# Taking the first four groups of products between the heads of the first search's second half, with a softmax for each half, and the second tile's row ahead

## The chip, the cores and the metric

The kernel runs on one core of a Trainium2 chip. The metric is the device time of one execution in microseconds (us), as the median of several runs. Engines: TensorE (PE), VectorE (DVE), ScalarE (ACT), GpSimd (POOL) and SyncE (SP). Each takes its own list of instructions in the order in which the program writes it, and waits on semaphores for the others.

## The reference, cut to what matters

A graph of 1250 nodes with 512 features and 21250 edges passes through four layers, each added to its input behind a layer norm: a graph convolution with batch norm and gelu, a memory layer with product keys, a second graph convolution, and one of eight 512 x 512 matrices per node. The change lies in the second:

```python
q = (x @ Wq + bq).reshape(-1, 8, 128)
q1, q2 = q[..., :64], q[..., 64:]
s1 = einsum('bhc,hnc->bhn', q1, keys[:, 0])      # 256 scores for each head
s2 = einsum('bhc,hnc->bhn', q2, keys[:, 1])
s1t, i1 = top_k(s1, 8);  s2t, i2 = top_k(s2, 8)
scores, best = top_k(all 64 sums of s1t and s2t, 8)
indices = (i1 * 256 + i2) at best                 # 8 heads x 8 rows of 65536
inner = einsum('bd,bhkd->bhk', x, w_down[indices])
vals = relu(inner) * softmax(scores)              # over the 8 of a head
out = einsum('bhk,bhkd->bd', vals, w_up[indices])
```

Each node needs 64 rows of `w_down` and 64 of `w_up`. The kernel holds them side by side, so that one gathered row is 4 KB.

## The kernel before

The nodes lie in 10 tiles of 128 (`NT`), a node to a partition. For each tile the memory layer has two stages.

The **search**. The tile's row is normalised (`y_stats`, `y_root`, `y_inv`, `y_norm`: VectorE and ScalarE in turn), TensorE flips it (`flip_y`, L1923), ScalarE copies it out of PSUM (`copy_yT`, L910). TensorE makes the queries of two heads at a time (`queries`, L1932), ScalarE copies them with their bias (`copy_q`, L948). TensorE makes a head's scores (L1943; L2096 in the first tile), ScalarE copies them (L955; L1038), VectorE finds the eight largest and their places (L1395 and L1400; L1544 to L1556). Then VectorE combines the heads and writes a list of indices (`idx`, L1449; L1598), ScalarE takes the exponentials (`exps`, L985), and VectorE divides by their sums (`softmax`, L1458 to L1462) to get `prob`.

The **groups**. GpSimd gathers the rows of a tile by its list (L702), 128 rows of 4 KB (512 KB) at a time, two gathers to a group, 32 groups to a tile (`NG`). The rows land in a ring of ten groups (`RING`); a slot is free again when TensorE has summed its group (`grp_done`). For each group VectorE multiplies the `w_down` halves by the normalised row `Y` and sums them into `inner` (two products, L1534, scaled by `prob`), ScalarE makes two diagonal matrices of the relu of `inner` (L1030), and TensorE sums diagonal times `w_up` half (L2081).

While a tile's groups run, the searches of the next tiles are spread between them: `Places` says ahead of which group `g` each engine does which step of a search. `FIRST` is the list for tile 1, whose search runs in the groups of tile 0; its steps with a negative `g` run ahead of group 0. Its queries stand at groups 0, 2, 6 and 8, head h's scores at 2h + 2, their copy one group later, and the maxima one group behind that. With sums at 19 its list of indices comes at group 25.

Tile 0's own search has nothing to hide behind. It is written out by hand. Its list of indices comes in two halves (`SHARES`), one for four heads each, and GpSimd starts to gather by the first. VectorE goes through the heads in pairs (`first_pair`): the even head from a copy that ScalarE made, the odd head straight from a PSUM bank `S1`. There is one such bank pair, so TensorE's scores for an odd head h wait until the places of head h - 2 are found:

```python
        if h == 1:
            pe.wait_ge(k.x1_done, 4)
        elif h % 2:
            pe.wait_ge(k.topk_done, h - 1)
```

On ScalarE this search is: `copy_q` for two heads, the copy of the even head's scores, four times over, with two gelus of the first layer (L886) behind the last `copy_q`; then `keep_y(0)` (L924), which writes `Y`, then the exponentials (L985), and the root of the out-degrees (L1052). A function of another kind (root, gelu, exponential) has an ACT_TABLE_LOAD in front of it. On TensorE it is `flip_y(0)`, four times queries and two heads' scores, then `flip_y(1)`.

Of the kernel before, what the change touches and what calls it, by code (L numbers as in the profile page):

```python
# [23 lines left out]
ALU = mybir.AluOpType  # L24
ACT = mybir.ActivationFunctionType
AX = mybir.AxisListType

P = 128
N = 1250
D = 512  # L30
E = 21250
NT = -(-N // P)
# [3 lines left out]
H = 8  # L36
NK = 256
HK = H * 8
# [30 lines left out]
GS = 2  # L69
SHARES = 2  # L70
NG = HK // GS
RING = 10
# [30 lines left out]
class Places:  # L103


    def __init__(self, y_stats, y_inv, y_norm, y_copy, y_keep, queries, q_lag, scores, s_lag, m_lag, sums):
        self.y_stats, self.y_root, self.y_inv, self.y_norm, self.y_flip = y_stats, y_stats, y_inv, y_norm, y_norm
        self.y_copy, self.y_keep = y_copy, y_keep
        self.queries, self.q_copy = queries, [q + q_lag for q in queries]
        self.scores = scores  # L110
        self.s_copy = [s + s_lag for s in scores]
        self.maxes = [s + s_lag + m_lag for s in scores]
        self.finds = [s + s_lag + m_lag + 1 for s in scores]
        self.sums, self.best, self.place, self.codes = sums, sums + 1, sums + 2, sums + 3
        self.match, self.rows, self.index, self.exps, self.softmax = sums + 4, sums + 5, sums + 6, sums + 5, sums + 11
# [2 lines left out]
STEADY = Places(-36, -32, -32, -28, 2, [8 * c - 28 for c in range(4)], 4, [4 * h - 24 for h in range(H)], 4, 3, 13)  # L118
LATER = {2 + 3 * i: 4 + i for i in range(NT - 4)}
W1_MEANS, W1_CENTRED, LATER_ADD = NG + 3, NG + 6, 3  # L120
FIRST = Places(-6, -4, -3, -1, 1, [0, 2, 6, 8], 1, [2 * h + 2 for h in range(H)], 1, 1, 19)
FINAL = Places(-36, -32, -32, -28, 2, [8 * c - 28 for c in range(4)], 4, [4 * h - 24 for h in range(H)], 4, 3, 13)
FINAL.codes, FINAL.match, FINAL.rows, FINAL.index = 15, 16, 16, 17
TABLES, ROUTES, ROUTED, HOSTS, LAST_HOST = 1, 4, 7, 12, 28
# [9 lines left out]
def groups_of(i):  # L134
    return NG if i < NT - 1 else NG_LAST
# [655 lines left out]
def act_program(act, k):  # L791
# [92 lines left out]
    def gelu(o, i0, i1):  # L884
        piece = k.outT[:, o * NPAD + i0 * P:o * NPAD + i1 * P]
        act.activation(piece, piece, ACT.Gelu, bias=k.bsc[:, FT + o:FT + o + 1],  # L886
                       scale=k.bsc[:, o:o + 1]).then_inc(k.gelu_done, 1)
# [20 lines left out]
    def copy_yT(i):  # L908
        act.wait_ge(k.yt_ready, i + 1)
        act.activation(k.yT[:, :], k.YT, copy).then_inc(k.yT_done, 1)  # L910
# [6 lines left out]
    def keep_y(i):  # L917
        if i >= 2:
            act.wait_ge(k.inner_ready, (i - 1) * NG)
        elif i:  # L920
            act.wait_ge(k.topk_done, H)
        else:
            act.wait_ge(k.x1_done, 4)
        act.activation(k.Y[i % 2], k.x[:, i * D:(i + 1) * D], ACT.Identity, bias=k.yco[:, i % 2 * 2 + 1:i % 2 * 2 + 2],  # L924
                       scale=k.yco[:, i % 2 * 2:i % 2 * 2 + 1]).then_inc(k.y_kept, 1)
# [52 lines left out]
    def keep_g(i):  # L978
        act.wait_ge(k.g_psum, i + 1)
        act.wait_ge(k.hco_ready, i + 1)  # L980
        act.activation(k.g[i % 3], k.TK[i % 2], copy, scale=k.hco[:, 0:1]).then_inc(k.g_kept, 1)

    def exps(i):
        act.wait_ge(k.exp_in, i + 1)
        act.activation(k.ex[:, :], k.sm[:, :], ACT.Exp).then_inc(k.exp_done, 1)  # L985

    def search_step(i, at, g):
# [14 lines left out]

    def tile(i):
        for g in range(groups_of(i)):
            if i and g == AfterTile(i).root:
                x_root(i - 1)
            if i and g == AfterTile(i).copy:
                copy_xf(i - 1)
            if i and g == AfterTile(i).keep:
                keep_g(i - 1)  # L1010
            for j, at, place in at_search(i, g):
                search_step(j, at, place)
            n = i * NG + g
            if n in WIDEN:
                widen(WIDEN[n])
            if n in SCALED:
                scale_sums(SCALED[n])
            if i == NT - 2 and g == TABLES:
                tables()
            if i == NT - 2 and g == ROUTED:  # L1020
                keep_routes()
            if i == NT - 1 and g == 0:
                act.wait_ge(k.routes_ready, 1)
            act.wait_ge(k.inner_ready, n + 1)
            act.wait_ge(k.grp_done, n + 1 - DB + RING)
            for s in range(GS):
                j = g * GS + s
                c = (n % DB) * GS + s
                to = k.ident[:, :] if i < NT - 1 else k.routes[:, j // WIDTH * P:(j // WIDTH + 1) * P]
                ins = act.activation(k.diag[:, c * P:(c + 1) * P], to, ACT.Relu,  # L1030
                                     scale=k.inner[:, j:j + 1])
            ins.then_inc(k.diag_ready, 1)

    def first_scores(h):
        act.wait_ge(k.s_ready, h + 1)
        if h >= 4:
            act.wait_ge(k.topk_done, h - 3)
        act.activation(k.sc[h // 2 % 2].rearrange("p (c n) -> p c n", c=2), k.S[:, :, 0:NK], copy).then_inc(k.sc_ready, 1)  # L1038

    y_root(0)  # L1040
    y_norm(0)
    copy_yT(0)
    for c in range(4):
        copy_q(0, c)
        if c == 3:
            gelu(2, 4, NT)
            gelu(3, 4, NT)
        first_scores(2 * c)
    keep_y(0)
    exps(0)  # L1050
    act.wait_ge(k.dego_ready, 1)
    act.activation(k.dsq[:, 2 * NT:3 * NT], k.deg[:, 2 * NT:3 * NT], ACT.Sqrt).then_inc(k.degosq_ready, 1)  # L1052
    for g in range(FIRST.y_root, 0):
        search_step(1, FIRST, g)
    for i in range(NT):
        tile(i)
    copy_xf(NT - 1)
# [43 lines left out]
def dve_program(dve, k):  # L1101
# [351 lines left out]
                                     ALU.mult, ALU.add).then_inc(k.rows_known, 1)  # L1453

    def softmax(i):
        dve.wait_ge(k.exp_done, i + 1)
        ex = k.ex[:, :].rearrange("p (h a) -> p h a", a=8)
        dve.tensor_reduce(k.ssum[:, 0:H], ex, AX.X, ALU.add)  # L1458
        dve.drain()
        dve.reciprocal(k.ssum[:, H:2 * H], k.ssum[:, 0:H])  # L1460
        dve.drain()
        dve.tensor_tensor(k.prob[:, (i % 2) * HK:(i % 2 + 1) * HK].rearrange("p (h a) -> p h a", a=8), ex,  # L1462
                          k.ssum[:, H:2 * H].unsqueeze(2).to_broadcast([P, H, 8]), ALU.mult)
        dve.drain()
        if i == NT - 1:
            dve.sem_inc(k.weights_known, 1)
# [10 lines left out]
    def search_step(i, at, g):  # L1477
# [22 lines left out]
        if g == at.softmax:  # L1500
            softmax(i)

    def tile(i):
        for g in range(groups_of(i)):
            n = i * NG + g
            if i and g == AfterTile(i).add:
                x_add(i - 1)
            if i and g == AfterTile(i).stats:
                x_stats(i - 1)
            if i and g == AfterTile(i).inv:  # L1510
                x_inv(i - 1)
            if n in UNIT_ADD:
                add_unit(UNIT_ADD[n])
            if n - LATER_ADD in LATER:
                add_gelu(LATER[n - LATER_ADD])
            if n == W1_CENTRED:
                center_w1()
            for j, at, place_ in at_search(i, g):
                search_step(j, at, place_)
            r = n % RING  # L1520
            if i == NT - 2 and g == GATHERED:
                keep_rows()
            if i == NT - 2 and g == WEIGHTED:
                keep_weights()
            if g == 0:
                if i < NT - 1:
                    dve.wait_ge(k.y_kept, i + 1)
                else:
                    dve.wait_ge(k.y_hosted, 2)
            dve.wait_ge(k.landed[r], (n // RING + 1) * (16 * GS))  # L1530
            for s in range(GS):
                j = g * GS + s
                row = k.slot[r * GS + s][:, 0:D]
                ins = dve.tensor_tensor_reduce(  # L1534
                    out=row, in0=row, in1=k.Y[i % 2] if i < NT - 1 else k.Yh[j // WIDTH],
                    scale=k.prob[:, (i % 2) * HK + j:(i % 2) * HK + j + 1], scalar=0.0, op0=ALU.mult, op1=ALU.add,
                    accum_out=k.inner[:, j:j + 1])
            ins.then_inc(k.inner_ready, 1)

    def first_pair(h):  # L1540
        dve.wait_ge(k.sc_ready, h // 2 + 1)
# [60 lines left out]
    y_inv(0)  # L1602
    for i in range(1, 4):
        add_gelu(i)
    for b in range(SHARES):
        first_pair(4 * b)
        first_pair(4 * b + 2)
        first_part(b)
    sums_of = k.best[:, :].rearrange("p (h a) -> p h a", a=8)
    dve.tensor_tensor(k.sm[:, :].rearrange("p (h a) -> p h a", a=8), sums_of,  # L1610
                      sums_of[:, :, 0:1].to_broadcast([P, H, 8]), ALU.subtract).then_inc(k.exp_in, 1)
    dve.sem_inc(k.sc_ready, H // 2)
    softmax(0)
    dve.wait_ge(k.degosq_ready, 1)
    dve.reciprocal(k.dri[:, 2 * NT:3 * NT], k.dsq[:, 2 * NT:3 * NT])
    dve.drain()
    for g in range(FIRST.y_stats, 0):
        search_step(1, FIRST, g)
    for i in range(NT):
        tile(i)  # L1620

# [126 lines left out]
def pe_program(pe, k):  # L1748
# [353 lines left out]
    for c in range(4):  # L2102
        queries(0, c)
        first_scores(2 * c)
        first_scores(2 * c + 1)
    for g in range(FIRST.y_flip, 0):
        search_step(1, FIRST, g)
    for i in range(NT):
        tile(i)

# [113 lines left out]
```

## Time and profile before

| | |
|---|---|
| median of 3 runs | 1150.19 us (1150.16 to 1151.8) |
| the profiled execution's own time | 1151.4 us |
| its span, first to last instruction | 1149.2 us |
| mean granted TensorE clock | 0.98 |
| busy share: PE, DVE, ACT, POOL | 94%, 75%, 39%, 59% |
| gathers: L702 on POOL | 628, 944 to 952 ns each |

The page cuts the span in 40 slices of 28.7 us. Tile 0's search and the first gathers lie at 195 to 258 us, in slices 6 to 8 counted from 0. In a timeline a row is: start, us, engine, line and operation, out<-in by names, count, and in brackets the engine's idle time before it and what ended that. A row with a count above one is the sum over the instructions merged into it, from the first one's start to the last one's end. Times are us from the span's start. The granted clock of 1.00 is 2.4 GHz, that of 0.50 is 1.2 GHz.

### The profile page before, as it was taken

Reading aid. Unit: us, or ns where it says so; the run is one execution under the profiler, and the core shown is the slowest. Engines: PE = TensorE matmul, PEld = TensorE weight load, DVE = VectorE, ACT = ScalarE, POOL = GpSimd, SP = SyncE. Lnnn points to the kernel's source line nnn. Section 1 sums busy time; section 2 is a strip of 40 time slices with the busy share of each in tenths; the row PEclk is TensorE's granted clock in tenths of the full one; section 3 lists DMA queues with packets and bytes.
Section 4 is the critical chain, followed back from the end, with each engine's and each line's share of the span. In section 5 each row is a group of like instructions: output and inputs, shape, how many; then the busy total and the mean of one; then the engine's idle time right before and its main releaser. Section 6 shows DMA issues by size and latency. Waiting matters only on the chain.

```text
span 1149.2 us, 15190 instructions
## 1 busy us (share of the span) xinstructions
PE 1086.0 (94%) x3724; PEld 579.5 (50%) x3725; DVE 862.7 (75%) x2753; ACT 453.5 (39%) x1119; POOL 677.9 (59%) x751
## 2 busy tenths in 40 slices
PE   7989998489999999999999999999999989998998
PEld 3568887355444554454444544544544434343543
DVE  6757766769989988789788789798798796664411
ACT  3731114344444544444434434434434333353222
POOL 2010004477677777777777776777776777777322
PEclk9989999889999999999999999999999999999899
DMA  8960011499999999999999999999999999994822
GB/s 319 406 261 2 2 31 81 156 410 385 384 408 400 409 409 409 408 409 408 409 408 409 409 408 409 408 409 409 408 409 380 410 409 409 409 406 151 287 83 89
DMA packets 108439, 379.96 MB, mean 331 GB/s; under 512 B 11850, under 2 KB 12656, under 8 KB 108228
## 3 DMA queue, kind: packets, MB, share of 16 engines
q0 software_dynamic: 92272, 334.49, 73.6%
q1 hardware_dynamic: 16084, 44.51, 10.4%
q8 instruction: 33, 0.54, 0.2%
q14 instruction: 50, 0.41, 0.1%
HBM read 351.88 MB, written 27.93 MB: 330 GB/s over the span
## 4 chain that ended last, share of the span: by engine, by line
PE 61%; DVE 14%; DMA 9%; POOL 6%; issue 4%; DVEq 2%; ACT 2%; SPq 0%; POOLq 0%; ACTq 0%
PE tr L2081 28%; DMA big<-in_wdu,idx 7%; PE acc L1861 6%; PE acc L1973 5%; POOL big L702 5%; PE acc L1932 4%; DVE big L1534 4%; PE acc L1943 3%; PE tr L2166 2%; PE acc L1792 2%; DMA AT<-in_wdu,idx 2%; PE acc L2166 2%; PE acc L1815 1%; POOL AT L702 1%; PE tr L1965 1%
## 5 line engine op out<-in xcount | busy, mean ns | idle before, releaser
L702 POOL DMA_INDIRECT big<-in_wdu,idx x504 | 475.7, 944 | 188.9 <-issue 137.6
L2081 PE MATMUL tr<-big,back 128*128 128x512 f32 x1008 | 463.7, 599 | 14.2 <-ACT back L1030 13.9
L1534 DVE CUSTOM_DVE_ANT_0 big<-big,acc,prob 128x512 f32<-128x512 f32 x504 | 353.9, 742 | 82.8 <-DMA big<-in_wdu,idx 80.7
L1030 ACT ACTIVATE back<-ident,inner 128x128 f32<-128x128 f32 x576 | 199.4, 393 | 407.9 <-DVE inner L1534 407.7
L2081 PEld LDWEIGHTS tr<-big,back 128*128 128x128 f32 x1008 | 184.2, 190 | 249.8 <-issue 196.6
L702 POOL DMA_INDIRECT AT<-in_wdu,idx x124 | 118.1, 952 | 41.6 <-issue 33.6
L2081 PE MATMUL tr<-AT,back 128*128 128x512 f32 x248 | 115.1, 598 | 1.5 <-ACT back L1030 1.4
L1534 DVE CUSTOM_DVE_ANT_0 AT<-AT,acc,prob 128x512 f32<-128x512 f32 x124 | 87.3, 743 | 23.1 <-DMA AT<-in_wdu,idx 22.7
L1861 PE MATMUL acc<-AT,big 128*128 128x256 f32 (+1 forms) x400 | 91.2, 379 | 0.0
L1973 PE MATMUL acc<-front 128*128 128x512 f32 x188 | 88.7, 597 | 0.6 <-issue 0.5
L1932 PEld LDWEIGHTS acc<-front 128*128 128x128 f32 x640 | 78.2, 195 | 19.1 <-issue 17.1
L1932 PE MATMUL acc<-front 128*128 128x128 f32 x640 | 81.0, 281 | 1.6 <-ACT front L910 1.4
L1861 PEld LDWEIGHTS acc<-AT,big 128*128 128x128 f32 x400 | 75.7, 194 | 7.3
L2081 PEld LDWEIGHTS tr<-AT,back 128*128 128x128 f32 x248 | 45.4, 190 | 59.4 <-issue 47.3
L673 POOL TENSOR_TENSOR AT<-AT,ident 128x128 f32<-128x128 f32 x10 | 4.8, 476 | 103.3 <-ACT AT L813 103.3
L1395 DVE MAX8 top<-back 128x8 f32<-128x256 f32 x144 | 53.8, 416 | 10.4 <-ACT back L955 10.4
L1400 DVE FIND_INDEX8 topi<-top,back 128x8 uint32<-128x256 f32 x144 | 58.5, 419 | 0.0
L1973 PEld LDWEIGHTS acc<-front 128*128 128x128 f32 x188 | 34.7, 190 | 43.2 <-issue 42.6
L1534 DVE DVE_READ_ACCUMULATOR2_ANT inner<- 128x1 f32 x628 | 52.2, 83 | 0.0
L1943 PE MATMUL acc<-front 64*128 64x256 f32 x288 | 50.6, 428 | 0.0
L955 ACT ACTIVATE back<-acc 128x512 f32<-128x512 f32 x72 | 42.1, 585 | 3.4 <-PE acc L1943 3.4
L1226 DVE TENSOR_SCALAR back<-big 128x320 f16 x88 | 22.9, 302 | 27.0 <-PE acc L1815 10.2
(334 smaller groups left out, 1082.5 us busy)
## 6 DMA issues: line engine op xcount, KB each, us to landing
sorted_rows<-big SPq DMA_DIRECT2D x33, 640.0 KB, 18.7
big<-in_we SPq DMA_DIRECT2D x8, 1024.0 KB, 13.7
big<-in_wdu,idx POOLq DMA_INDIRECT x504, 10.2
x<-sorted_rows SPq DMA_DIRECT2D x13, 257.5 KB, 2.8
x<-in_x SPq DMA_DIRECT2D x1, 2304.0 KB
big<-in_xt SPq DMA_DIRECT2D x2, 1024.0 KB, 8.8
front<-in_wq SPq DMA_DIRECT2D x1, 2048.0 KB, 7.8
AT<-in_wdu,idx POOLq DMA_INDIRECT x124, 10.3
```

The source lines that it names most:

```text
L702: pool.indirect_dma_start(out=k.slot[r * GS + s], out_offset=None, in_=k.wdu_d, in_offset=bass.IndirectOffsetOnAxis(ap=k.idx[i % 2][:, j:j ...
L955: act.activation(k.sc[h % 2].rearrange("p (c n) -> p c n", c=2), k.S[:, :, 0:NK], copy).then_inc(k.sc_ready, 1)
L1030: ins = act.activation(k.diag[:, c * P:(c + 1) * P], to, ACT.Relu, scale=k.inner[:, j:j + 1])
L1395: dve.max(k.top[:, c * HK + h * 8:c * HK + h * 8 + 8], k.sc[h % 2][:, c * NK:(c + 1) * NK])
L1400: ins = dve.max_index(k.topi[:, c * HK + h * 8:c * HK + h * 8 + 8], k.top[:, c * HK + h * 8:c * HK + h * 8 + 8], k.sc[h % 2][:, c * NK:(c ...
L1534: ins = dve.tensor_tensor_reduce(out=row, in0=row, in1=k.Y[i % 2] if i < NT - 1 else k.Yh[j // WIDTH], scale=k.prob[:, (i % 2) * HK + j:(i ...
L1861: ins = pe.matmul(k.banks[2 + p % 4][:, 0:n], k.xw[:, t * D + o * P:t * D + (o + 1) * P], k.AT[:, t * NPAD + c0:t * NPAD + c0 + n], start= ...
L1932: ins = pe.matmul(k.Q[:, (h % 4) * P:(h % 4 + 1) * P], k.wq[:, f * H * P + h * P:f * H * P + (h + 1) * P], k.yT[:, f * P:(f + 1) * P], sta ...
L1943: ins = pe.matmul(k.S[:, c, 0:NK], k.qT[half, (h % 4) * P:(h % 4 + 1) * P], k.keys[half, h * NK:(h + 1) * NK], start=True, stop=True)
L1973: return pe.matmul(bank, counts[:, t % 4 * P:(t % 4 + 1) * P], k.g[j % 3], start=begin, stop=end)
L2081: ins = pe.matmul(k.O[i % 2], k.diag[:, c:c + P], row, start=(g == 0 and s == 0), stop=(g == groups_of(i) - 1 and s == GS - 1))
L2166: return pe.matmul(k.E[part], k.zT[part][:, f * P:(f + 1) * P], k.big[:, bass.ds(b * (FT * D) + f * D, D)], start=(f == 0), stop=(f == FT ...
```

## The change

`FIRST` loses its steps ahead of group 0 and its first two queries. They are written out by hand, inside the first search:

- VectorE does `y_stats(1)` and `y_inv(1)` and the reciprocal of the out-degrees' root ahead of the first pair of heads. ScalarE does `y_root(1)`, that root, and `y_norm(1)` ahead of the first `copy_q`.
- ScalarE does `copy_yT(1)` behind the last `copy_q(0, 3)`, ahead of the two gelus and of the copy of head 6's scores. Behind that copy it does `copy_q(1, 0)` and `copy_q(1, 1)`, then `keep_y(0)` and the exponentials of the first half.
- TensorE does `flip_y(1)` and the first two `queries` of tile 1 behind the scores of head 7.
- VectorE takes the groups' products out into a function, `products`. Its order in tile 0 is: heads 0 to 3, first half of the list, subtraction, heads 4 and 5, softmax of the first half, groups 0 and 1, heads 6 and 7, groups 2 and 3, second half of the list, subtraction, softmax of the second half, then the loop from group 4.
- ScalarE does the exponentials of the second half ahead of group 4's diagonals.

The diff, cut:

```diff
-FIRST = Places(-6, -4, -3, -1, 1, [0, 2, 6, 8], 1, [2 * h + 2 for h in range(H)], 1, 1, 19)
+FIRST = Places(None, None, None, None, 1, [None, None, 6, 8], 1, [2 * h + 2 for h in range(H)], 1, 1, 19)
+FIRST_GROUPS = (2, 4)
...
+    def first_exps(b):
+        half = slice(b * HK // SHARES, (b + 1) * HK // SHARES)
+        act.wait_ge(k.exp_in, b + 1)
+        act.activation(k.ex[:, half], k.sm[:, half], ACT.Exp).then_inc(k.exp_done, 1)
...
     def tile(i):
         for g in range(groups_of(i)):
+            if i * NG + g == FIRST_GROUPS[1]:
+                first_exps(1)
...
     y_root(0)
     y_norm(0)
     copy_yT(0)
+    y_root(1)
+    act.wait_ge(k.dego_ready, 1)
+    act.activation(k.dsq[:, 2 * NT:3 * NT], k.deg[:, 2 * NT:3 * NT], ACT.Sqrt).then_inc(k.degosq_ready, 1)
+    y_norm(1)
     for c in range(4):
         copy_q(0, c)
         if c == 3:
+            copy_yT(1)
             gelu(2, 4, NT)
             gelu(3, 4, NT)
         first_scores(2 * c)
+    for c in range(2):
+        copy_q(1, c)
     keep_y(0)
-    exps(0)
-    act.wait_ge(k.dego_ready, 1)
-    act.activation(k.dsq[:, 2 * NT:3 * NT], k.deg[:, 2 * NT:3 * NT], ACT.Sqrt).then_inc(k.degosq_ready, 1)
-    for g in range(FIRST.y_root, 0):
-        search_step(1, FIRST, g)
+    first_exps(0)
...
     for i in range(1, 4):
         add_gelu(i)
-    for b in range(SHARES):
-        first_pair(4 * b)
-        first_pair(4 * b + 2)
-        first_part(b)
...
+    dve.drain()
+    y_stats(1)
+    y_inv(1)
     dve.wait_ge(k.degosq_ready, 1)
     dve.reciprocal(k.dri[:, 2 * NT:3 * NT], k.dsq[:, 2 * NT:3 * NT])
...
+    def first_softmax(b):
+        hh = H // SHARES
+        half = slice(b * hh * 8, (b + 1) * hh * 8)
+        ex = k.ex[:, half].rearrange("p (h a) -> p h a", a=8)
+        dve.wait_ge(k.exp_done, b + 1)
+        dve.tensor_reduce(k.ssum[:, b * hh:(b + 1) * hh], ex, AX.X, ALU.add)
...
+    def less_best(b):
+        half = slice(b * HK // SHARES, (b + 1) * HK // SHARES)
+        sums_of = k.best[:, half].rearrange("p (h a) -> p h a", a=8)
+        dve.tensor_tensor(k.sm[:, half].rearrange("p (h a) -> p h a", a=8), sums_of,
+                          sums_of[:, :, 0:1].to_broadcast([P, H // SHARES, 8]), ALU.subtract).then_inc(k.exp_in, 1)
+
+    first_pair(0)
+    first_pair(2)
+    first_part(0)
+    less_best(0)
+    first_pair(4)
+    first_softmax(0)
+    for g in range(FIRST_GROUPS[0]):
+        products(0, g)
+    first_pair(6)
+    dve.sem_inc(k.sc_ready, H // 2)
+    for g in range(*FIRST_GROUPS):
+        products(0, g)
+    first_part(1)
+    less_best(1)
+    first_softmax(1)
     for i in range(NT):
         tile(i)
...
         first_scores(2 * c)
         first_scores(2 * c + 1)
-    for g in range(FIRST.y_flip, 0):
-        search_step(1, FIRST, g)
+    flip_y(1)
+    for c in range(2):
+        queries(1, c)
```

## Rows read from the trace of the kernel before

**Rows 1.** The page: GB/s moved in 40 equal slices of the span

```profile
GB/s 319 406 261 2 2 31 81 156 410 385 384 408 400 409 409 409 408 409 408 409 408 409 409 408 409 408 409 409 408 409 380 410 409 409 409 406 151 287 83 89
```

**Rows 2.** Windows: busy us (x instructions) by engine, clock, DMA share, GB/s

```profile
238.00:239.00 1.00, 1.00 (x7) 1.00 (x6) 0.29 (x2) 0.00 (x0) 0.94 (x1) 0.51 1.03 414
...
245.76:303.33 57.57, 55.31 (x211) 28.13 (x210) 53.00 (x177) 24.13 (x64) 39.18 (x42) 1.00 1.02 397
...
300.00:308.00 8.00, 7.43 (x31) 4.26 (x32) 7.79 (x20) 5.45 (x15) 3.80 (x5) 1.00 0.99 366
...
400.00:860.00 460.00, 452.73 (x1435) 217.64 (x1435) 389.16 (x1259) 194.93 (x512) 338.94 (x359) 1.00 1.03 409
```

**Rows 3.** Timeline of POOL, gathers: start, us, engine, line, [idle before <- releaser]

```profile
217.53 1.19 POOL L702 DMA_INDIRECT big<-in_wdu,idx  x1 [11.69 <-DVE idx L1598]
...
303.60 0.94 POOL L702 DMA_INDIRECT big<-in_wdu,idx  x1 [3.29 <-DVE idx L1449]
```

**Rows 4.** Timeline of DVE, first search and first groups

```profile
204.50 0.75 DVE L1544 MAX8 top<-back 128x8 f32<-128x256 f32 x2 [5.71 <-ACT back L1038]
...
219.42 0.42 DVE L1556 FIND_INDEX8 topi<-top,acc 128x8 uint32<-128x256 f32 x1
...
223.19 0.42 DVE L1570 TENSOR_TENSOR back<-top 128x256 f32<-128x256 f32 x1
...
228.42 0.22 DVE L1610 TENSOR_TENSOR sm<-best 128x64 f32<-128x64 f32 x1
228.96 0.22 DVE L1458 TENSOR_REDUCE ssum<-sm 128x8 f32<-128x64 f32 x1 [0.32 <-ACT sm L985]
...
229.53 0.23 DVE L1462 TENSOR_TENSOR prob<-sm,ssum 128x64 f32<-128x64 f32 x1
...
232.86 0.75 DVE L1534 CUSTOM_DVE_ANT_0 big<-big,acc,prob 128x512 f32<-128x512 f32 x1
...
235.54 0.74 DVE L1534 CUSTOM_DVE_ANT_0 big<-big,acc,prob 128x512 f32<-128x512 f32 x1
...
245.76 0.76 DVE L1395 MAX8 top<-back 128x8 f32<-128x256 f32 x2 [7.47 <-ACT back L955]
```

**Rows 5.** Timeline of ACT, the same stretch

```profile
202.70 0.63 ACT L948 ACTIVATE front<-acc,par 128x128 f32<-128x128 f32 x2 [2.14 <-PE acc L1932]
...
214.94 1.28 ACT L886 ACT_TABLE_LOAD   x1
216.24 1.95 ACT L886 ACTIVATE outT<-outT,bsc 128x768 f32<-128x768 f32 x2
218.09 0.57 ACT L1038 ACTIVATE back<-acc 128x512 f32<-128x512 f32 x1
218.56 0.77 ACT L924 ACTIVATE acc<-x,yco 128x512 f32<-128x512 f32 x1
219.35 1.28 ACT L985 ACT_TABLE_LOAD   x1
228.67 0.26 ACT L985 ACTIVATE sm<-sm 128x64 f32<-128x64 f32 x1 [8.04 <-DVE sm L1610]
...
234.90 0.60 ACT L910 ACTIVATE front<-acc 128x512 f32<-128x512 f32 x1 [1.21 <-PE acc L1923]
```

**Rows 6.** Timeline of PE, the same stretch

```profile
219.99 1.23 PE L2096 MATMUL acc<-front 64*128 64x256 f32 x4 [4.57 <-DVE topi L1556]
233.75 1.12 PE L1923 MATMUL acc<-ident,front 128*128 128x128 f32 x4 [12.53 <-ACT front L914]
235.55 3.68 PE L1932 MATMUL acc<-front 128*128 128x128 f32 x16 [0.69 <-ACT front L910]
...
242.50 1.95 PE L1932 MATMUL acc<-front 128*128 128x128 f32 x16
...
252.36 1.98 PE L2081 MATMUL tr<-big,back 128*128 128x512 f32 x4 [0.27 <-ACT back L1030]
```

**Rows 7.** Waits of DVE from 245 to 303.4 us: total, times, longest

```profile
DVE top L1395 <- ACT back L955: 10.4, 3, 7.5
```

More of the change, by code:

```diff
@@ L108, in __init__ @@
         self.y_copy, self.y_keep = y_copy, y_keep
-        self.queries, self.q_copy = queries, [q + q_lag for q in queries]
+        self.queries, self.q_copy = queries, [None if q is None else q + q_lag for q in queries]
         self.scores = scores
@@ L981, in keep_g @@
         act.activation(k.g[i % 3], k.TK[i % 2], copy, scale=k.hco[:, 0:1]).then_inc(k.g_kept, 1)
+    def first_exps(b):
+        half = slice(b * HK // SHARES, (b + 1) * HK // SHARES)
+        act.wait_ge(k.exp_in, b + 1)
+        act.activation(k.ex[:, half], k.sm[:, half], ACT.Exp).then_inc(k.exp_done, 1)
     def exps(i):
-        act.wait_ge(k.exp_in, i + 1)
+        act.wait_ge(k.exp_in, i + SHARES)
         act.activation(k.ex[:, :], k.sm[:, :], ACT.Exp).then_inc(k.exp_done, 1)
@@ L1455, in softmax @@
     def softmax(i):
-        dve.wait_ge(k.exp_done, i + 1)
+        dve.wait_ge(k.exp_done, i + SHARES)
         ex = k.ex[:, :].rearrange("p (h a) -> p h a", a=8)
@@ L1501, in search_step, with products @@
             softmax(i)
+    def products(i, g):
+        n = i * NG + g
+        r = n % RING
+        if g == 0:
+            if i < NT - 1:
+                dve.wait_ge(k.y_kept, i + 1)
+            else:
+                dve.wait_ge(k.y_hosted, 2)
+        dve.wait_ge(k.landed[r], (n // RING + 1) * (16 * GS))
+        for s in range(GS):
+            j = g * GS + s
+            row = k.slot[r * GS + s][:, 0:D]
+            ins = dve.tensor_tensor_reduce(
+                out=row, in0=row, in1=k.Y[i % 2] if i < NT - 1 else k.Yh[j // WIDTH],
+                scale=k.prob[:, (i % 2) * HK + j:(i % 2) * HK + j + 1], scalar=0.0, op0=ALU.mult, op1=ALU.add,
+                accum_out=k.inner[:, j:j + 1])
+        ins.then_inc(k.inner_ready, 1)
     def tile(i):
-        for g in range(groups_of(i)):
+        for g in range(0 if i else FIRST_GROUPS[1], groups_of(i)):
             n = i * NG + g
@@ L1519, in tile @@
                 search_step(j, at, place_)
-            r = n % RING
             if i == NT - 2 and g == GATHERED:
@@ L1524, in tile @@
                 keep_weights()
[L1525 to L1538, printed above, removed]
+            products(i, g)
     def first_pair(h):
@@ L1604, in dve_program @@
         add_gelu(i)
-    for b in range(SHARES):
-        first_pair(4 * b)
-        first_pair(4 * b + 2)
-        first_part(b)
[L1609 to L1613, printed above, removed]
+    dve.drain()
+    y_stats(1)
+    y_inv(1)
     dve.wait_ge(k.degosq_ready, 1)
     dve.reciprocal(k.dri[:, 2 * NT:3 * NT], k.dsq[:, 2 * NT:3 * NT])
-    dve.drain()
-    for g in range(FIRST.y_stats, 0):
-        search_step(1, FIRST, g)
+    def first_softmax(b):
[4 more added lines that the diff above has]
+        dve.tensor_reduce(k.ssum[:, b * hh:(b + 1) * hh], ex, AX.X, ALU.add)
+        dve.drain()
+        dve.reciprocal(k.ssum[:, H + b * hh:H + (b + 1) * hh], k.ssum[:, b * hh:(b + 1) * hh])
+        dve.drain()
+        dve.tensor_tensor(k.prob[:, half].rearrange("p (h a) -> p h a", a=8), ex,
+                          k.ssum[:, H + b * hh:H + (b + 1) * hh].unsqueeze(2).to_broadcast([P, hh, 8]), ALU.mult)
+        dve.drain()
+    def less_best(b):
[18 more added lines that the diff above has]
+    first_softmax(1)
     for i in range(NT):
@@ L2105, in pe_program @@
         first_scores(2 * c + 1)
-    for g in range(FIRST.y_flip, 0):
-        search_step(1, FIRST, g)
+    flip_y(1)
+    for c in range(2):
+        queries(1, c)
     for i in range(NT):
```

## The prediction

> **What bounds the kernel now.** I read the page's forty slices first. The reader is to see that from the middle of the run on, 408 to 410 GB/s stand in nearly every slice [rows 1], and the window from 400 to 860 us confirms it with 409 GB/s at a DMA share of 1.03 [rows 2]. There the transfers set the pace. A microsecond by which the gathers start later, or stop, in the first tile is therefore not won back behind it: it moves the end. So I looked for the places where the gathers stop. GpSimd's timeline shows two long ones. It waits 11.69 us for the first list of indices, until 217.53, and 3.29 us for the second tile's list, until 303.60 [rows 3]. At the second the transfers run dry: 366 GB/s from 300 to 308 us [rows 2]. The second tile's list ends a chain on VectorE: from the first search of tile 1 at 245.76 to that list VectorE is busy 53.00 of 57.57 us [rows 2], with 2.9 us of waits (10.4 in all, less the 7.5 that end at 245.76) [rows 4, 7]. So what decides is **when VectorE begins group 4 of the first tile, with its search step at 245.76**, and what it does in the 22 groups behind it, which the change leaves as they are.
>
> **The change, part by part.**
>
> *The second tile's row goes ahead.* Before, 3.1 us lie between the end of the softmax (229.53 + 0.23 = 229.76) and the first product at 232.86 [rows 4]: the statistics, two roots, the normalisation. Now VectorE does this in its gap of 5.71 us ahead of 204.50 [rows 4]. ScalarE has a gap of 2.14 ahead of 202.70 [rows 5]; it takes a normalisation of 0.77 (the same form as L924) and two roots (of the variance, and of the out-degrees) that I put at 0.26 each, the price of the small exponential: 1.3 us [rows 5]. Cost nothing; without that cover the first search would be late by at most 1.3. That the first list comes at 217.53 stays.
>
> *The copy of the second tile's row is put ahead of the scores of heads 6 and 7.* This is the part that I hold to be decisive. The copy of yT waits for the transposes of tile 1; TensorE issues these behind the scores of head 7; those wait until VectorE has found the places of head 5 (rows 6: 219.99, after 4.57 us idle). Before, only these last scores waited. Now ScalarE itself stands at the copy, and queued behind it are both gelus, the copy of head 6's scores, two query copies of tile 1, the keeping of Y, and the first half's exponentials, for which VectorE waits before its first product. Step by step, with each duration from its row:
> - Head 5's places end at 219.42 + 0.42 = 219.84 [rows 4]; the new subtraction puts 0.22 ahead of them: 220.06. TensorE follows after 0.15 with the scores, 1.23, and the transposes, 1.12 [rows 6]: 222.6. Copy 0.60 [rows 5]: 223.2.
> - Table of the gelu 1.28 and 0.02, the gelus 1.85 from start to start, the scores' copy 0.57 [rows 5]: 226.9. Meanwhile the first queries of tile 1, 3.68 at the lower clock [rows 6], end at 226.9 too. Copy 0.63 [rows 5]: 227.6.
> - The second queries: 3.68 at the granted clock of 0.50 (1.2 GHz), or 1.95 at 1.00 (2.4 GHz) [rows 6]. The row of the first kind ended with the rise (0.51 still in 238 to 239) [rows 2], after TensorE had worked without a break since 235.55; here its work is broken by 0.7 us before and after the first queries. So I take 3.68: 231.3. With 1.95 it would be 229.6.
> - Copy 0.67 with its start, keeping Y 0.77, table of the exponential 1.30, exponential 0.26 [rows 5]: 234.3 (or 232.6).
>
> *Two softmaxes and the four groups.* On VectorE from there: half a softmax 0.87 (228.96 to 229.76 and a drain; a half costs hardly less than a whole), 235.2; two groups 2.68 (232.86 to 235.54), 237.9; heads 6 and 7 3.35 (219.84 to 223.19), 241.3; two groups, 244.0; the second half of the search 5.23 (223.19 to 228.42), 249.2; subtraction 0.22, exponential 0.32 to its arrival, softmax 0.87: 250.6 [rows 4]. So the first group begins at 235.2 and not at 232.86: **it isn't earlier, it is 2.4 us later**, and group 4's step begins at 250.6 instead of 245.76. That is 4.8 us late; neighbouring rows overlap by about 0.1 (218.09 starts before 216.24 + 1.95 is over) [rows 5], so I take 4.7. With the second queries at the higher clock: 3.0. These are the two ends of what is on the path.
>
> *What is taken away.* VectorE's wait of 7.47 us before 245.76 [rows 4] came from tile 1's queries, which stood between groups 0 to 3 on TensorE. It goes; in its place VectorE waits from 220.1 to 234.3 us, 14 us, for exponentials. The sum above holds both. Two new waits stand beside it: tile 1's first scores wait for the increment behind heads 6 and 7, and keeping tile 1's Y waits for head 7's places, with group 1's diagonals behind it. Both come at 241.3; scores and copy, at most 1.23 and 0.57, are there well before VectorE asks for them at 250.6. If they were not, VectorE's gap at 245.76 would be back.
>
> *What hides nothing.* No DMA is added, moved or taken away. The first twenty gathers fill the ring without a sum; at 512 KB and 409 GB/s [rows 1], 1.28 us each, they end at 217.53 + 25.6 = 243, and group 0 is summed by about 241. Group 14's gathers wait for group 4, which is late, so GpSimd will stand a few microseconds around 255. That alone is not the price: it stands again for tile 1's list, and that comes 4.7 later. Nor does less work on TensorE help: it has a gap of 0.27 before group 5's sums at 252.36 [rows 6], so VectorE's later waits of 2.9 us do not stem from the backlog, but from two queries and their scores between a group's sums, which stay there.
>
> **Sum.** The profiled execution took 1151.4 us with a span of 1149.2, 1.2 above the median of 1150.19. With 4.7 its own time would be 1156.1; on the median I forecast **1154.9 us**.
>
> One price differs from the Trainium skill. The rows show ScalarE's next instruction 0.02 us after a table load of 1.28 (214.94 + 1.28 to 216.24) [rows 5]. The page "ScalarE: Activation LUTs", section "What ACT_TABLE_LOAD costs", adds a drain of about 1.38 us to each switch; with its figure the two loads that now lie on the path would cost 2.8 more, an estimate of 7.5 in all. This trace shows no such drain.
>
> **Rivals.**
> - *Higher clock for the second queries*: 3.0 late, 1153.2. For it: TensorE restarts at 220.2 already, some 7 us before these queries. Against: the breaks.
> - *TensorE's relief takes VectorE's waits of 2.9 us away*: 4.7 - 2.9 = 1.8 late, 1152.0; with the higher clock 0.1, 1150.3. For it: TensorE is busy 55.31 of 57.57 us there [rows 2], and does a transpose and two queries fewer. Against: the gap of 0.27.
> - *The delay is swallowed later*: 1150.2. It needs spare transfer time behind 303; rows 1 show only the slices with 400 and 380 GB/s.
> - *TensorE sets the pace of the first tile*, so it ends sooner. Group 0's sums would begin at about 236.9 in place of some 239 (235.55 + 3.68), without the 1.95 of queries among them: some 4 us sooner, of which the transfers can use the 3.29 for which GpSimd stands: 1146.9. It decides if group 4's products are ready before TensorE has summed group 3, about 250. Against: by the sum above they begin only behind 250.6, and VectorE's 53.00 of 57.57 leave no room.
> - *ScalarE stands still behind each load*, once more for about as long as the load's own row, 1.28: 2.6 more for the two, 7.3 late, 1157.5. Against: the 0.02.
>
> **How the numbers follow.** Lower clock 0.42, higher clock 0.22, relief 0.16, swallowed 0.07, TensorE's pace 0.10, drain 0.03. About 0.2%, 2.3 us, is what a measurement here can tell from no change. Slower by more: 0.42 + 0.22 + 0.03 = 0.67; within: relief and swallowed, 0.23; faster: 0.10. The range goes from 1150.6, inside the relief case, to 1156.2, the 4.8 without overlaps on the profiled execution's own time: it leaves out the pace case, the drain, and part of the swallowed ones. For slower alone it is 1152.6 to 1156.2.
>
> **What would show it.** ScalarE idle from about 215 to 222.5 ahead of the copy of yT, with the gelu's table behind it and not before; VectorE idle some 14 us ahead of the first half's sums at 234; first product at 235, group 4's step at 250.6; GpSimd's wait for tile 1's list ending at 308 and longer than 3.29. The forecast is wrong if the copy of yT does not wait for head 5, if the waits of 2.9 us go, or if the list of tile 1 comes before 304.

## The result and the profile after

| | before | after |
|---|---|---|
| median | 1151.34 us (8 runs, 1148.0 to 1154.84) | 1155.66 us (8 runs, 1153.46 to 1159.03) |
| profiled execution, its span | 1151.4, 1149.2 | 1155.9, 1154.0 |
| mean granted TensorE clock | 0.98 | 0.977 |

The ratio is 1.0047, with an interval of 1.0034 to 1.0061: slower by 4.3 us. A second set of runs (below) gave 1.0021 [1.0004, 1.0039].

In the profiled execution of the changed kernel the first gather issued at 216.01 and not at 217.53 [rows 3]. That place differs from one execution to the next (217.47 in the second profile of the same kernel), so from here on places are counted from the first gather. First GpSimd's timeline of the kernel after:

```profile
216.01 1.19 POOL L703 DMA_INDIRECT big<-in_wdu,idx  x1 [11.63 <-DVE idx L1613]
...
254.75 0.94 POOL L703 DMA_INDIRECT big<-in_wdu,idx  x1 [2.31 <-PE tr L2121]
...
262.49 0.94 POOL L703 DMA_INDIRECT big<-in_wdu,idx  x1 [2.65 <-PE tr L2121]
...
306.38 0.94 POOL L703 DMA_INDIRECT big<-in_wdu,idx  x1 [2.05 <-DVE idx L1460]
```

The second tile's first gather stands 90.37 us behind the first; before it stood at 303.60 - 217.53 = 86.07 [rows 3]. It is 4.30 later, as much as the medians lie apart. VectorE's timeline after:

```profile
232.78 0.19 DVE L1630 TENSOR_REDUCE ssum<-sm 128x4 f32<-128x32 f32 x1 [14.35 <-ACT sm L987]
...
233.68 0.75 DVE L1526 CUSTOM_DVE_ANT_0 big<-big,acc,prob 128x512 f32<-128x512 f32 x1 [0.20 <-issue]
...
248.79 0.76 DVE L1406 MAX8 top<-back 128x8 f32<-128x256 f32 x2
...
260.47 0.76 DVE L1406 MAX8 top<-back 128x8 f32<-128x256 f32 x2 [0.96 <-ACT back L956]
...
267.10 0.75 DVE L1406 MAX8 top<-back 128x8 f32<-128x256 f32 x2 [1.93 <-ACT back L956]
```

The old wait of 7.47 ahead of group 4's step [rows 4] is gone and one of 14.35 ahead of the first softmax has come. The first product stands at +17.67 (before 232.86 - 217.53 = +15.33), group 4's step at +32.78 (before +28.23). What VectorE waits for is on ScalarE's timeline after:

```profile
220.88 0.60 ACT L911 ACTIVATE front<-acc 128x512 f32<-128x512 f32 x1 [7.48 <-PE acc L1963]
221.50 1.28 ACT L887 ACT_TABLE_LOAD   x1
222.79 1.94 ACT L887 ACTIVATE outT<-outT,bsc 128x768 f32<-128x768 f32 x2
224.64 0.57 ACT L1046 ACTIVATE back<-acc 128x512 f32<-128x512 f32 x1
225.35 0.62 ACT L949 ACTIVATE front<-acc,par 128x128 f32<-128x128 f32 x2
229.91 0.63 ACT L949 ACTIVATE front<-acc,par 128x128 f32<-128x128 f32 x2 [3.94 <-PE acc L1972]
230.42 0.78 ACT L925 ACTIVATE acc<-x,yco 128x512 f32<-128x512 f32 x1
231.22 1.28 ACT L987 ACT_TABLE_LOAD   x1
232.52 0.23 ACT L987 ACTIVATE sm<-sm 128x32 f32<-128x32 f32 x1
```

Between its instructions ScalarE stands still twice, both times for TensorE: 7.48 us for the transposes of tile 1, 3.94 for the second queries. TensorE's timeline after, with the two queries of tile 1 at the half clock (3.78 and 3.75 us) and group 4's sums at the full one (1.98), and the windows in and behind the second queries:

```profile
218.57 1.23 PE L2136 MATMUL acc<-front 64*128 64x256 f32 x4 [4.67 <-DVE topi L1571]
219.73 1.11 PE L1963 MATMUL acc<-ident,front 128*128 128x128 f32 x4
221.53 3.78 PE L1972 MATMUL acc<-front 128*128 128x128 f32 x16 [0.69 <-ACT front L911]
226.12 3.75 PE L1972 MATMUL acc<-front 128*128 128x128 f32 x16 [0.81 <-ACT front L949]
...
252.49 1.98 PE L2121 MATMUL tr<-big,back 128*128 128x512 f32 x4 [2.63 <-ACT back L1038]
```

```profile
226.00:230.00 4.00, 3.75 (x16) 3.49 (x16) 0.00 (x0) 0.09 (x1) 2.87 (x4) 0.50 1.01 385
231.00:233.00 2.00, 0.00 (x0) 0.00 (x0) 0.19 (x1) 1.72 (x3) 1.51 (x2) 1.00 1.03 414
```

The granted clock rises to 1.00 only behind the second queries, which end at 229.87, while TensorE stands idle.

The windows of the kernel after (busy us by engine, granted clock, DMA share, GB/s) and the page's row of GB/s:

```profile
236.00:240.00 4.00, 3.67 (x4) 1.06 (x4) 3.85 (x15) 0.26 (x1) 2.93 (x4) 0.50 1.03 411
260.00:280.00 20.00, 20.00 (x78) 10.01 (x77) 17.16 (x57) 9.29 (x25) 12.58 (x14) 1.00 0.90 317
300.00:308.00 8.00, 6.97 (x30) 3.59 (x29) 7.74 (x17) 4.30 (x12) 5.04 (x5) 1.00 1.01 402
300.00:320.00 20.00, 18.97 (x73) 9.80 (x73) 18.82 (x55) 11.54 (x30) 14.04 (x14) 1.00 0.98 369
400.00:860.00 460.00, 452.95 (x1435) 217.83 (x1435) 388.99 (x1262) 196.00 (x514) 341.75 (x362) 1.00 1.03 409
```

```profile
GB/s 321 407 255 2 1 64 48 185 393 346 383 409 401 403 409 408 409 409 409 409 410 409 409 409 409 409 409 409 408 409 394 409 409 410 408 383 174 271 71 84
```

Two windows of the kernel before, to set beside these:

```profile
260.00:280.00 20.00, 20.00 (x80) 10.06 (x79) 17.72 (x58) 9.07 (x23) 14.44 (x16) 1.00 1.00 372
300.00:320.00 20.00, 19.43 (x77) 10.28 (x78) 19.33 (x61) 11.47 (x30) 12.75 (x15) 1.00 1.00 369
```

At 236 to 240 the granted clock is 0.50 again: it fell while TensorE stood idle for 6.02 us, and group 0's sums run at the half level too. The transfers lose more at 260 to 280 us: 317 GB/s, where the kernel before has 372. The sag at the second tile's list only moves with the list: at 300 to 308, where the kernel before had 366 [rows 2], there are 402, and over 300 to 320 both have 369. From the middle on both stand at 409 [rows 1, 2], and little of what was lost is won back: the last product of all groups is 832.13 us behind the first gather, before 828.47, 3.7 later.

### The profile page after: what moved, and what is told of

It reads as the page before. It is cut to its first block, busy times and chain, and to the rows that moved or that the text cites. A ratio compares the mean times of both kernels' runs of the same rounds, so it can differ in the third digit from the quotient of the medians.

```text
span 1154.0 us, 15198 instructions
## 1 busy us (share of the span) xinstructions
PE 1092.1 (95%) x3724; PEld 582.4 (50%) x3725; DVE 862.4 (75%) x2757; ACT 453.5 (39%) x1120; POOL 680.5 (59%) x751
## 4 chain that ended last, share of the span: by engine, by line
PE 60%; DVE 13%; DMA 10%; POOL 7%; issue 5%; DVEq 2%; ACT 2%; SPq 0%; POOLq 0%; ACTq 0%
PE tr L2121 27%; DMA big<-in_wdu,idx 10%; PE acc L1901 6%; POOL big L703 5%; PE acc L2013 5%; PE acc L1972 5%; DVE big L1526 4%; PE acc L1983 3%; PE tr L2207 2%; PE acc L1832 2%; PE acc L2207 2%; PE acc L1855 1%; PE tr L2005 1%; POOL AT L703 1%; PE tr L1855 1%
## 5 line engine op out<-in xcount | busy, mean ns | idle before, releaser
L1972 PEld LDWEIGHTS acc<-front 128*128 128x128 f32 x640 | 79.8, 199 | 19.7 <-issue 17.7
L751 POOL DMA_INDIRECT out<-outT,back x13 | 12.8, 985 | 51.6 <-DVEq L1773 48.2
```

Source lines behind the costliest of these rows:

```text
L1972: ins = pe.matmul(k.Q[:, (h % 4) * P:(h % 4 + 1) * P], k.wq[:, f * H * P + h * P:f * H * P + (h + 1) * P], k.yT[:, f * P:(f + 1) * P], sta ...
```

## Experiments

Each kernel was timed in five rounds against the kernel before, in three sets: after_again, copy_behind, queries_behind and exps_first (before: 1151.47 us), then row_only, clock_kept and gap_filled (1151.68), then both_kept on another chip (1151.1). Each ratio is to the kernel before of its own set. The four places are us behind the first gather, from the timelines of one profile each. All ratios lie within 0.5%; the places show the order of things more sharply than the times do.

| kernel | first product | group 4's step | second tile's first gather | last product | median us | ratio |
|---|---|---|---|---|---|---|
| before | 15.33 | 28.23 | 86.07 | 828.47 | 1151.34 | |
| changed | 17.67 | 32.78 | 90.37 | 832.13 | 1155.66 | 1.0047 [1.0034, 1.0061] |
| after_again | 17.68 | 32.82 | 90.42 | 833.40 | 1154.86 | 1.0021 [1.0004, 1.0039] |
| copy_behind | 17.67 | 32.78 | 92.30 | 834.62 | 1155.0 | 1.0024 [1.0008, 1.0039] |
| queries_behind | 12.35 | 27.44 | 85.99 | 828.71 | 1151.32 | 0.9996 [0.9985, 1.0007] |
| exps_first | 6.71 | 24.62 | 82.90 | 826.15 | 1148.96 | 0.9978 [0.9964, 0.9992] |
| row_only | 12.45 | 20.05 | 80.91 | 826.47 | 1149.14 | 0.9977 [0.9962, 0.9992] |
| clock_kept | 14.71 | 29.82 | 89.28 | 831.46 | 1153.39 | 1.0018 [1.0005, 1.0031] |
| gap_filled | 17.68 | 32.79 | 90.36 | 832.82 | 1154.54 | 1.0022 [1.0011, 1.0032] |
| both_kept | 14.72 | 29.84 | 87.70 | 830.04 | 1151.5 | 1.0003 [0.9989, 1.0016] |

**The changed kernel once more** (after_again), beside the kernels of its set.

> The changed kernel itself, once more, to size the slowdown. Times are counted from GpSimd's first gather: before, group 4's search step comes at +28.2 us and the second tile's first gather at +86.1; in the changed kernel at +32.8 and +90.4. By the queue theory (ScalarE stands at the copy of the second tile's row, with its queries and the first half's exponentials behind) the time is 3.7 to 4.5 us above before: 4.3 at the second tile's list, of which the last product had lost 0.65 again. If instead something behind the first tile adds to it, the time is 5 us or more above before, and the way from the second tile's list to the last product is longer than before's 742 us.

The places repeat to 0.1 us. The time does not repeat as well: its executions run from 1150.65 to 1158.89, four of the twelve between 1150.6 and 1151.4. By the medians the kernel is 3.4 us slower, by the ratio 2.4; both lie below the 3.7 to 4.5 that were expected, and further from the 5 or more that a loss behind the first tile would have added up to.

**Only the copy of yT behind the gelus and head 6's copy** (copy_behind):

```diff
         if c == 3:
-            copy_yT(1)
             gelu(2, 4, NT)
             gelu(3, 4, NT)
         first_scores(2 * c)
+    copy_yT(1)
```

> The changed kernel with only the copy of yT moved behind both gelus and the copy of head 6's scores; the query copies stay ahead of the exponentials. Queue theory, as the prediction has it: the gelus and that copy ended together with the first queries, so the second queries at the lower clock still end 14 us after the first gather and the exponentials come no sooner than 0.3 us: group 4's step at +32.5 to +32.8, and the time is the changed kernel's. Rival, that the gelus with their table are what delays: 3 us sooner, about 1 us above before.

Group 4's step stays at +32.78. So the place of this copy alone costs nothing at this step: with the gelus and head 6's copy ahead of it ScalarE uses the time in which it otherwise stood, and the exponentials still come when the query copies in front of them are through. This profile, an execution of 1158.7 us, shows a second loss. TensorE's timeline, then VectorE's, then the windows of copy_behind:

```profile
228.54 3.75 PE L1972 MATMUL acc<-front 128*128 128x128 f32 x16 [0.81 <-ACT front L949]
...
254.91 3.78 PE L2121 MATMUL tr<-big,back 128*128 128x512 f32 x4 [4.03 <-ACT back L1038]
```

```profile
264.58 0.75 DVE L1406 MAX8 top<-back 128x8 f32<-128x256 f32 x2 [2.65 <-ACT back L956]
```

```profile
254.00:258.00 4.00, 3.09 (x4) 1.41 (x5) 3.91 (x14) 1.87 (x5) 0.00 (x0) 0.50 1.02 407
258.00:262.00 4.00, 4.00 (x16) 2.44 (x15) 3.83 (x13) 0.69 (x2) 2.11 (x3) 0.77 0.43 123
```

After an idle 4.03 us TensorE does group 4's sums at a granted clock of 0.50, in 3.78 us in place of 1.98. VectorE then waits 2.65 in place of 0.96 for the next scores, the ring comes free later, the transfers fall to 123 GB/s, and the second tile's list is 92.30 - 90.37 = 1.9 us later still. The median, 1155.0, is that of the changed kernel all the same.

**Only the query copies behind the exponentials** (queries_behind):

```diff
-    for c in range(2):
-        copy_q(1, c)
     keep_y(0)
     first_exps(0)
+    for c in range(2):
+        copy_q(1, c)
```

> The changed kernel with the two query copies of tile 1 moved behind the first half's exponentials on ScalarE; the copy of yT stays where it is. Queue theory: the exponentials come 5.2 us sooner (scores' copy, 0.78, 1.30, 0.23), group 4's step at +27.6, the second tile's first gather at about +85, and the time is back at before's, 0 to 1 us below. Rival, the order on VectorE (groups between the heads and two softmaxes cost more by themselves): group 4's step stays above +30 and the time 2 us or more above before. Rival, TensorE's lower clock: the sums and queries run as slowly as in the changed kernel, and the time stays 2 us or more above before.

VectorE's, TensorE's and GpSimd's timelines of queries_behind:

```profile
229.80 0.18 DVE L1630 TENSOR_REDUCE ssum<-sm 128x4 f32<-128x32 f32 x1 [9.03 <-ACT sm L987]
```

```profile
249.49 3.68 PE L2121 MATMUL tr<-big,back 128*128 128x512 f32 x4 [3.15 <-ACT back L1038]
```

```profile
304.34 0.94 POOL L703 DMA_INDIRECT big<-in_wdu,idx  x1 [2.04 <-DVE idx L1460]
```

The wait shrinks from 14.35 to 9.03, group 4's step comes 5.34 sooner, and the whole loss is gone. The order on VectorE, groups between the heads and two softmaxes, is thus not what cost the time. The list, expected at about 85, stands at 85.99: here too TensorE did group 4's sums mostly at the half clock, 3.68 us behind an idle 3.15, and VectorE then waited 1.91 for the next scores where the changed kernel waited 0.96.

**All of tile 1 behind the exponentials** (exps_first):

```diff
         if c == 3:
-            copy_yT(1)
             gelu(2, 4, NT)
             gelu(3, 4, NT)
         first_scores(2 * c)
-    for c in range(2):
-        copy_q(1, c)
     keep_y(0)
     first_exps(0)
+    copy_yT(1)
+    for c in range(2):
+        copy_q(1, c)
```

> The changed kernel with ScalarE's order gelus, head 6's scores, keeping of Y, first half's exponentials, and only then the copy of yT and the two query copies. Queue theory: the exponentials end about 3.4 us after the first gather, VectorE has its first half's weights at about +4.5 and then waits for rows instead (group 0's at +6 to +12, group 1's at +8.5 to +14, as 4.5 to 10.2 us from issue to landing); group 4's step at +22.5 to +28, the second tile's first gather at +80 to +86, and 1 to 4 us below before. Rival, the order on VectorE: still 2 us or more above before. Rival, TensorE's pace in the first tile: no better than the version with only the queries behind.

VectorE's and TensorE's timelines and the windows of exps_first:

```profile
221.83 0.19 DVE L1630 TENSOR_REDUCE ssum<-sm 128x4 f32<-128x32 f32 x1 [0.95 <-ACT sm L987]
...
225.17 0.75 DVE L1526 CUSTOM_DVE_ANT_0 big<-big,acc,prob 128x512 f32<-128x512 f32 x1 [2.63 <-DMA big<-in_wdu,idx]
```

```profile
246.78 3.43 PE L2121 MATMUL tr<-big,back 128*128 128x512 f32 x4 [4.17 <-ACT back L1038]
```

```profile
260.00:280.00 20.00, 20.00 (x73) 9.21 (x72) 17.71 (x58) 9.84 (x25) 15.04 (x16) 1.00 1.03 409
280.00:300.00 20.00, 18.45 (x67) 9.20 (x65) 19.19 (x72) 7.53 (x21) 15.01 (x15) 1.00 1.03 409
```

The groups are now taken as early as the rows land: VectorE's wait is no longer for ScalarE but for the gathered rows. The transfers do not sag any more, though group 4's sums run mostly at the half clock here too, and the kernel is 2.5 us faster than the one before.

**The row ahead without the early groups** (row_only): the kernel before, with the statistics, norm, flip and first two queries of tile 1 moved as in the change, but one softmax and no group between the heads. Its own part on ScalarE, behind the first search (the copy of yT and the first query copy stand ahead of the exponentials, only the second query copy behind them):

```diff
     keep_y(0)
+    copy_yT(1)
+    copy_q(1, 0)
     exps(0)
...
-    for g in range(FIRST.y_root, 0):
-        search_step(1, FIRST, g)
+    copy_q(1, 1)
```

> The kernel before, with the second tile's row, its flip and its first queries ahead as in the change, but without the early groups on VectorE and with one softmax for all heads; the query copies stand behind the exponentials. If the early groups gain nothing and the row ahead does it all: first product about 12.3 us after the first gather, group 4's search step at 21 to 23.6, the second tile's first gather at 78.5 to 81 (its floor is the first tile's 64 gathers, 79.6), the transfers don't stop, and the time is 2.5 to 4 us below the kernel before. Rival, that the early groups are what gains: the time is about that of the kernel before (ratio 0.999 to 1.001).

VectorE's timeline and the windows of row_only:

```profile
231.05 0.75 DVE L1537 CUSTOM_DVE_ANT_0 big<-big,acc,prob 128x512 f32<-128x512 f32 x1 [0.21 <-issue]
...
238.65 0.75 DVE L1398 MAX8 top<-back 128x8 f32<-128x256 f32 x2 [2.17 <-ACT back L955]
```

```profile
260.00:280.00 20.00, 20.00 (x80) 10.15 (x77) 19.54 (x64) 9.12 (x22) 14.98 (x16) 1.00 1.03 408
280.00:300.00 20.00, 18.23 (x66) 9.05 (x65) 19.30 (x70) 8.47 (x23) 15.35 (x16) 1.00 1.03 410
300.00:320.00 20.00, 20.00 (x71) 9.68 (x70) 18.31 (x63) 11.79 (x30) 15.12 (x17) 1.00 1.03 409
```

Group 4's step stands at +20.05, sooner than in any other kernel and than the 21 to 23.6 expected, and the time is that of exps_first. So the gain that the change holds lies in the row ahead; the early groups are not needed for it. Both kernels meet the same limit, transfers at 408 to 410 GB/s in the windows shown: row_only's list is written at +77.2, so GpSimd never stands for it, and yet the last product comes no sooner (826.47) than in exps_first (826.15), where GpSimd stands until +82.90. Early groups without the row ahead were not tried.

**TensorE kept at work ahead of head 7's scores** (clock_kept); the products are read by nothing:

```diff
         first_scores(2 * c)
+        if c == 3:
+            unread(k.TK[0], k.wq[:, 0:D], 5)
         first_scores(2 * c + 1)
```

> The changed kernel, with five matrix products that nothing reads put on TensorE between head 6's and head 7's first scores, so that TensorE has work until head 7's. If the price of ScalarE's new order is made of TensorE's half clock (second queries 3.75 us instead of 1.95): the second queries take 1.95, the exponentials come about 2.9 us sooner, group 4's search step starts about 29.9 us after the first gather (32.8 in the changed kernel), the second tile's first gather about 87.5 (90.4), and the time is 2 to 3 us below the changed kernel's, still 0.5 to 1.5 above the kernel before. Rival, that the clock makes no difference at this place: 32.8 and 90.4 stay, and the time is the changed kernel's (ratio 1.002 to 1.005).

TensorE's timeline of clock_kept:

```profile
220.97 2.05 PE L1972 MATMUL acc<-front 128*128 128x128 f32 x16 [0.69 <-ACT front L911]
225.31 2.02 PE L1972 MATMUL acc<-front 128*128 128x128 f32 x16 [2.29 <-ACT front L949]
...
249.95 3.78 PE L2121 MATMUL tr<-big,back 128*128 128x512 f32 x4 [4.03 <-ACT back L1038]
```

Both queries run at the full clock and group 4's step comes 2.96 sooner, as expected (29.9). The list, expected at 87.5, came at 89.28: here again TensorE had idled 4.03 us ahead of group 4's sums and did them in 3.78. The time, expected 0.5 to 1.5 us above the kernel before, is 1.7 above it.

**The gap ahead of group 4's sums filled** (gap_filled), on the changed kernel:

```diff
+            if n == FIRST_GROUPS[1]:
+                unread(k.G[0], k.wq[:, 0:D], 3)
```

> The changed kernel, with three matrix products that nothing reads on TensorE ahead of group 4's wait for its diagonals. If the changed kernel's scatter comes from TensorE's clock falling in that gap (2.6 us in two profiles without a fall, 4.0 us in one with it): the second tile's first gather stays at 90.4 us after the first, no execution near 1159, and the median is up to 1 us below the changed kernel's. Rival, that the scatter has another source: the same spread as the changed kernel's, 1150.5 to 1159.

TensorE's timeline of gap_filled:

```profile
255.12 1.98 PE L2123 MATMUL tr<-big,back 128*128 128x512 f32 x4 [1.25 <-ACT back L1038]
```

Group 4's sums take 1.98, and the list stands at +90.36. The median is 0.3 below after_again's, and executions of 1156.63 and 1157.65 remain. None reaches 1158, where after_again had two of twelve; but the executions around 1151 are gone too. That the fall in the gap makes the scatter is not decided by it.

**Both sets of products** (both_kept): those of clock_kept and of gap_filled in one kernel.

> The changed kernel with both sets of products that nothing reads: five between head 6's and head 7's first scores, three ahead of group 4's wait for its diagonals. If the clock's two prices are separate (2.9 us at the second queries, 1.8 in the gap ahead of group 4's sums, where the first set alone left a gap of 4.03 and sums of 3.78): group 4's step 29.8 us after the first gather, group 4's sums in 1.98, the second tile's first gather about 87.5 (86.1 in the kernel before, 89.3 with the first set alone), no execution near 1159, time about 1.3 us over the kernel before, ratio 1.000 to 1.0015. Rival, that it is not the clock but the order of the sums that makes this wait: the second tile's first gather stays at 89.3, ratio about 1.002.

TensorE's and GpSimd's timelines of both_kept:

```profile
227.81 2.02 PE L1972 MATMUL acc<-front 128*128 128x128 f32 x16 [2.29 <-ACT front L949]
...
252.46 1.98 PE L2123 MATMUL tr<-big,back 128*128 128x512 f32 x4 [1.26 <-ACT back L1038]
```

```profile
306.62 0.94 POOL L703 DMA_INDIRECT big<-in_wdu,idx  x1 [3.29 <-DVE idx L1460]
```

The list stands at +87.70 (expected 87.5) and the ratio is 1.0003. Against clock_kept's 89.28 this gives the fall in the gap a price of 1.6 us at the list; copy_behind against the changed kernel gave 1.9.

## Where the prediction failed, and what held

The sum of the path held. The cause that the prediction put first did not, and that the time came out near the forecast is due to the sum, which held both paths, and not to that cause.

**The sum held, step by step.** It is moved onto the first gather here, by taking off 217.53. Head 7's scores: +2.7 predicted, +2.56 measured (218.57 - 216.01). End of the copy of yT: +5.7 and +5.47. End of the second queries: +13.8 and +13.86. End of the exponentials: +16.8 and +16.74. First product: +17.7 and +17.67. Group 4's step: 4.7 late and 4.55. Second tile's list: 4.7 late and 4.30. Time: 4.7 later and 4.3. The early groups began later than before, as the prediction said.

**The choice of 3.68 for the second queries was right for the profiled executions** (3.75), against the rival of the higher clock, but the reason given for it, the breaks of 0.7 us, is not borne out, and the margin was small. The breaks were there (0.69 and 0.81), and the clock rose all the same: the second queries end at 229.87, and from 231 to 233 the granted clock is 1.00. That it rose behind them and not in them was luck as far as the prediction goes. clock_kept shows what the rival is worth when it does come about: 2.96 at group 4's step, more than the 1.7 put on it. The second queries give 1.7 of it, the scores and transposes 1.0 (the copy of yT ends at 220.31 + 0.60 - 216.43 = +4.48 in place of +5.47), and the first queries 0.2; the rest of their gain is hidden behind the gelus.

**The step that failed is which instruction was called decisive.** The prediction put the loss on the copy of yT ahead of head 6's and 7's scores ("the part that I hold to be decisive"). copy_behind takes exactly that away, and group 4's step stays at +32.78. The working had the reason in it: the gelus and head 6's copy end at 226.9, and "meanwhile" the first queries of tile 1 end at 226.9. These were two paths of one length (the trace after: head 6's copy ends at 225.21, the first queries at 225.31), and the copy's place decides over one of them alone. The two query copies ahead of the exponentials lie on both, and queries_behind, which moves only them, takes back the whole loss: group 4's step at +27.44, ratio 0.9996.

**The size of the time was set on a low base.** 1154.9 was 1150.19 + 4.7. Eight runs of the kernel before gave 1151.34, later sets 1151.47, 1151.68 and 1151.1. So with the increment 0.4 too large and the base about 1.2 too low, 1155.66 lies 0.8 above the forecast, near the top of the range. The increment is less sure than this: in the second set the slowdown is 3.4 us by the medians and 2.4 by the ratio, about half of the 4.7, with four of its twelve executions near 1151, where the first set has none. The sum had no term for such executions.

**A cost was missing, one that comes and goes.** No term stood for TensorE falling to its half clock between group 3's and group 4's sums. It is worth 1.6 to 1.9 us at the list in copy_behind and clock_kept. It was absent from both profiles of the changed kernel, so its share in that kernel's median is not known.

**The rivals.** That TensorE's relief takes VectorE's waits away falls: these waits remain, 0.96 and 1.93, together 2.9 as before. That the delay is swallowed later falls: of 4.30 at the list 3.66 are left at the last product. That TensorE sets the pace of the first tile falls: it idled 2.63 ahead of group 4's sums. That ScalarE stands still behind each table load falls: 221.50 + 1.28 = 222.78, and the gelus start at 222.79. The Trainium skill (the page "ScalarE: Activation LUTs", section "What ACT_TABLE_LOAD costs") adds a drain of about 1.38 us to each switch; the trace disagrees, by the same two rows.

**What should have shown it.** ScalarE idle to about 222.5: 220.88, which is 222.4 with the 1.52 of the earlier start. VectorE's idle 14: 14.35. GpSimd's wait for the second tile's list ending at 308: 306.38, which is 307.9. The same wait "longer than 3.29": wrong, 2.05. GpSimd had already been held up at the ring (2.31 at 254.75, 2.65 at 262.49; before, the longest such wait there was 1.85), so part of the delay had been taken ahead of the list.

What stays open: the two sets of the changed kernel differ (1.0047 and 1.0021, intervals that only just overlap), and the cluster of its executions around 1151 has no profile. That these are executions in which the clock rose sooner would fit (their mean clock is 0.981 to 0.982, that of the executions above 1158 is 0.976 to 0.977), all the more as in the profiles it rises just behind the second queries; it was not shown.

## What to carry to other kernels

When work for a later stage is moved ahead, put it in each engine's queue behind the instruction that the current stage waits for. Here two copies of 0.6 us, ahead of a 0.23 us exponential, put it behind another engine's 8 us of work, and the first product came 5.3 us later than with the copies behind it (+17.67 and +12.35). A copy ahead costs only what it makes the engine wait beyond its other waits: the copy of yT cost nothing at this step. Where two chains in a sum end at the same time, neither is decisive alone: name what stands behind both.

## What the runs showed of the hardware

- What TensorE's half clock costs depends on which of the slowed instructions lie on the path. Head 7's scores, the transposes and both queries took 4.4 us longer at 1.2 than at 2.4 GHz (1.23, 1.11, 3.78 and 3.75 us against 0.70, 0.66, 2.05 and 2.02 in clock_kept); 2.96 of this came through to group 4's step.
- In the changed kernel's profile the granted clock rose from 0.50 to 1.00 behind two queries of 3.78 and 3.75 us with 0.81 us between them, and was back at 0.50 when group 0's sums began after 6.02 us of idling.
- Group 4's sums took 1.98 us behind an idle gap of 2.63 (both profiles of the changed kernel), and 1.98 with products that nothing reads in the gap and 1.25 idle. They took 3.43 to 3.78 behind gaps of 3.15 (queries_behind), 4.03 (twice) and 4.17 (exps_first). In the changed kernel's profile the gap was the shorter because group 1's sums ahead of it had still run partly at the half clock (3.38); where these took 1.98 (copy_behind), the gap was longer and the clock fell behind it.
- Useless products on TensorE, put into both gaps, brought the second tile's list from 90.37 to 87.70 us behind the first gather, with nothing else moved. The ratio went from 1.0021 to 1.0003, in two sets and with intervals that overlap ([1.0004, 1.0039] and [0.9989, 1.0016]), so the gain in time is less sure than that at the list.
